# Attention and top-k experts on one core: a later turn of the selection, later copies of the second expert, another order at the end, and identity matmuls in the last sequence

## What is computed

```python
x = _layernorm(x + attention(x, W_key, W_query, W_value, W_proj))   # 16 causal heads of 16
x = _layernorm(x + ffn(x, router_w, w1, b1, w2, b2))
# ffn, for each sequence and each of 8 experts:
scores = softmax(x @ router_w.T)                 # over the experts
gate_vals, sel_idx = top_k(scores_t, capacity)   # capacity 129 of 512 tokens
tokens = x[b_idx, sel_idx]
h = gelu(tokens @ w1 + b1)                       # 256 -> 1024
y = h @ w2 + b2                                  # 1024 -> 256
out = zeros.at[b_idx, sel_idx].add(y * gate_vals[..., None])
```

## Time and profile before

| what | value |
|---|---|
| median of three runs | 898.7 us (894.87, 898.70, 898.88) |
| the profiled execution | 894.26 us; its span 892.5 us, 1.8 us lie around it |
| busy share of the span | PE 92%, DVE 68%, ACT 60%, POOL 52% |
| granted TensorE clock, mean | 0.979 of full |
| attention, until the last scores' turn | about 0 to 409 us |
| end of the last sequence and hand-over | 409 to 480 us |
| experts, steady | 480 to 846 us |
| the end | 846 to 892.5 us |

### The profile page before, as it was taken

How to read it: one execution, slowest core, us unless ns; L and a number is a source line. 1 busy time by engine, 2 the same in 40 slices (tenths; PEclk the granted TensorE clock), 3 DMA queues, 4 the chain that set the end, 5 groups by cost and what they waited for, 6 DMA issues and landing times.

```text
span 892.5 us, 17252 instructions
## 1 busy us (share of the span) xinstructions
PE 821.0 (92%) x5908; PEld 615.5 (69%) x5908; DVE 606.6 (68%) x2067; ACT 532.7 (60%) x1048; POOL 468.0 (52%) x640
## 2 busy tenths in 40 slices
PE   4779999999999999998778999999999999999994
PEld 3534454454645454433258999999999999999993
DVE  5668777788788778899858854546464554646466
ACT  2247767667586766666647445555565656555546
POOL 6458565666655565344658356445444444545343
PEclk9779999999999999999899999999999999999998
DMA  4863434536352424610253223335243342613275
GB/s 144 221 191 112 133 107 151 155 107 185 123 149 95 159 91 156 192 64 11 89 199 109 30 44 60 91 83 145 40 103 69 53 129 40 150 28 52 31 208 188
DMA packets 89574, 100.12 MB, mean 112 GB/s; under 512 B 8592, under 2 KB 82960, under 8 KB 89360
## 3 DMA queue, kind: packets, MB, share of 16 engines
q1 hardware_dynamic: 72128, 77.66, 27.8%
q0 software_dynamic: 12368, 16.52, 11.4%
q10 hardware_dynamic: 4992, 4.85, 1.8%
HBM read 65.38 MB, written 33.23 MB: 110 GB/s over the span
## 4 chain that ended last, share of the span: by engine, by line
PE 72%; DVE 14%; ACT 6%; issue 3%; POOL 1%; DMA 1%; SPq 1%; ACTq 1%; DVEq 0%; POOLq 0%
PE y_ps L1434 22%; PE h_ps L1416 18%; PE av_ps L816 7%; PE st_ps L784 5%; DVE n_ps L648 5%; PE n_ps L799 5%; PE stage_ps L835 3%; PE stage_ps L877 3%; PE stage_ps L843 3%; PE tp_ps L1389 2%; ACT pt L539 1%; DVE nmax L648 1%; DVE best_at L182 1%; DVE row_pool L184 1%; DVE nm L680 1%
## 5 line engine op out<-in xcount | busy, mean ns | idle before, releaser
L648 DVE CUSTOM_DVE_ANT_0 n_ps<-n_ps,tri 128x512 f32<-128x512 f32 (+3 forms) x512 | 238.6, 519 | 72.5 <-PE n_ps L799 70.5
L539 ACT ACTIVATE pt<-st_ps 128x512 f32<-128x512 f32 x320 | 184.4, 602 | 60.5 <-PE st_ps L784 45.5
L1434 PE MATMUL y_ps<-w_parts,h_hi 128*128 128x256 f32 (+1 forms) x1152 | 215.8, 281 | 2.0 <-POOL h_lo L1187 1.6
L1226 ACT ACTIVATE g<-h_ps,b 128x384 f32<-128x384 f32 (+1 forms) x192 | 104.1, 542 | 164.8 <-PE h_ps L1416 138.4
L1434 PEld LDWEIGHTS y_ps<-w_parts,h_hi 128*128 128x128 f32 (+1 forms) x1152 | 172.6, 177 | 5.9 <-issue 1.9
L1416 PE MATMUL h_ps<-tt_hi,w_parts 128*128 128x384 f32 (+1 forms) x768 | 169.7, 323 | 3.7 <-issue 2.0
L1198 POOL DMA_INDIRECT acc<-y,tok_no x61 | 98.1, 1608 | 140.7 <-DVE y L1342 132.7
L1326 DVE TENSOR_TENSOR h_lo<-g,h_hi 128x384 fp32r<-128x384 f32 (+1 forms) x176 | 90.1, 513 | 115.4 <-ACT h_hi L1231 95.6
L468 POOL TENSOR_SCALAR_AFFINE_SELECT pt<-pt 128x256 f32<-128x256 f32 (+1 forms) x320 | 109.8, 361 | 105.4 <-ACT pt L539 104.6
L1434 PE MATMUL y_ps<-w_parts,h_lo 128*128 128x256 f32 (+1 forms) x576 | 161.5, 280 | 0.0
L784 PE MATMUL st_ps<-w_parts 99*128 99x512 bf16 (+3 forms) x512 | 125.7, 307 | 17.5 <-ACT pt L539 15.9
(11 more groups left out here) (209 smaller groups left out, 1091.0 us busy)
## 6 DMA issues: line engine op xcount, KB each, us to landing
w_parts<-part_d SPq DMA_DIRECT2D x186, 128.0 KB, 2.8
w_raw<-in_w SPq DMA_DIRECT2D x16, 1024.0 KB
part_d<-w_raw SPq DMA_DIRECT2D x96, 128.0 KB, 2.2
w_raw<-in_xt SPq DMA_DIRECT2D x8, 512.0 KB, 4.2
res<-in_x SPq DMA_DIRECT2D x8, 512.0 KB, 4.7
x<-res SPq DMA_DIRECT2D x8, 512.0 KB, 3.3
acc<-res SPq DMA_DIRECT2D x8, 512.0 KB, 5.1
fin<-acc SPq DMA_DIRECT2D x4, 512.0 KB, 4.5
```

What stands on the lines that cost most here:

```text
L539: nc.scalar.activation(pt[:, slot % PT_RING, n % UP, :], st_ps[at % ST_RING][:, :], ACT.Exp, scale=S_SCALE).then_inc(exp_done, 1)
L648: ins = nc.vector.tensor_tensor_reduce(out=src[:, h, :], in0=src[:, h, :], in1=mask, scale=-1.0, scalar=-BIG_NEG, op0=ALU.add, op1=ALU.min ...
L1226: nc.scalar.activation(g[:, at % G_RING, 0:cols], h_ps[at % H_RING][:, 0:cols], ACT.Gelu, bias=b1[:, e, n:n + 1]).then_inc(g_done, 1)
L1434: ins = nc.tensor.matmul(y_ps[at % Y_RING][0:rows, 0:C], x[:, q % 2, m, toks], w[e % 2][:, m, :], start=i == 0, stop=i == len(terms) - 1)
```

## The change

Five edits, all in the tables that order the lists, and one new group of instructions.

1. `picked`, `joined` and `fetch` of the early selection go from place 3 to place 7 of the turn behind the last sequence.
2. In the last sequence's turn `lexp` goes from (2, 9) to (3, 8) and `score` from (3, 2) to (3, 9).
3. Expert 1's two copies on ScalarE go from places 1 and 12 to 24 and 25; the rest of its first weight (four VectorE operations, L714 before) moves from that turn to the experts' list, where each piece stands ahead of a piece of `low2`. The load of expert 2's first weight follows it.
4. 40 fp32 matmuls of the identity by itself into a free bank stand ahead of ten `st` stages (2 each) and ahead of `onorm` 2 and 3, `ot` 0 and 1 and `proj` 0 (4, 6, 5, 2, 3) of the last sequence. Their result is not read.
5. At the end the loads of sequences 0, 1, 2 stand ahead of those of 3, 4, 5, the `norm` stages stand elsewhere, and the three `spot` stages are spread over the job.

```diff
+HUM = {("onorm", 2): 4, ("onorm", 3): 6, ("ot", 0): 5, ("ot", 1): 2, ("proj", 0): 3}
+HUM.update({("st", n): 2 for n in range(30, 40)})
...
-NEXT_CUT_AT, NEXT_LOW_AT = ((B, 1), (B, 12)), (B, 11)
-PICK_AT = ((B - 2, 33), (B - 2, 35), (B, 3))
+NEXT_CUT_AT = ((B, 24), (B, 25))
+SCORE_AT = {'lexp': (3, 8), 'score': (3, 9)}
+PICK_AT = ((B - 2, 33), (B - 2, 35), (B, 7))
...
         for stage, b, n in steps():
+            if b == B - 1 and (stage, n) in HUM:
+
+                pe.wait_ge(max_done, B * NU)
+                for _ in range(HUM[stage, n]):
+                    nc.tensor.matmul(n_ps[0][:, 0:P], ident[:, :], ident[:, :], start=True, stop=True)
...
-FINISH += [((NQ - 2, 8), "load", b) for b in (0, 1, 2)]
-FINISH += [((NQ - 1, 0), "norm", 0), ((NQ - 1, 4), "norm", 1)]
...
+FINISH += [((NQ - 2, 8), "load", b) for b in (0, 1, 2) + ON_CHIP]
+FINISH += [((NQ - 2, 8), "norm", 0), ((NQ - 2, 9), "norm", 1), ((NQ - 1, 4), "norm", 2)]
...
             for e in range(1, E):
-                for stage in ("low1", "low2") if e > 1 else ("low2",):
+                for stage in ("low1", "low2"):
...
-        load_w1(2)
```

More of the change, by code:

```diff
@@ L144, in steps @@
                 for gg, kk, stage, ahead, n in STAGES:
+                    if i == B - 1:
+                        gg, kk = SCORE_AT.get(stage, (gg, kk))
                     if (gg, kk) == (g, k) and 0 <= i + ahead < B and (i, stage, n) not in STARTED:
@@ L164, in steps @@
                     yield "cut", 1, NEXT_CUT_AT.index((i, place))
-                if (i, place) == NEXT_LOW_AT:
-                    yield "low", 1, 0
                 if (i, place) == PICK_AT[2]:
@@ L709, in _ @@
                 logits(b)
-            elif stage == "low":
-                hi, lo = weight_parts(ahead, "w1", 1)
-                dve.wait_ge(ahead["w1_top"], 2 * PIECES)
-                for piece in range(PIECES):
-                    nc.vector.tensor_tensor(piece_of(lo, "w1", piece), piece_of(ahead["w1_raw"], "w1", piece),
-                                            piece_of(hi, "w1", piece).bitcast(F32), ALU.subtract).then_inc(ahead["w1_cut"], 1)
             elif stage == "halved":
@@ L935 @@
 ON_CHIP = CHUNKS[JOBS[NQ - 1][1]]
-FINISH = [((NQ - 2, 0), "load", 6), ((NQ - 2, 1), "load", 7)] + [((NQ - 2, 2), "load", b) for b in ON_CHIP]
-FINISH += [((NQ - 2, 4), "norm", 6), ((NQ - 2, 7), "norm", 7)]
-FINISH += [((NQ - 2, 8), "load", b) for b in (0, 1, 2)]
-FINISH += [((NQ - 1, 0), "norm", 0), ((NQ - 1, 4), "norm", 1)]
-ON_CHIP_AT = [((NQ - 2, 0), "spot", b) for b in ON_CHIP]
-ON_CHIP_AT += [((NQ - 1, 7), "spread", ON_CHIP[0]), ((NQ - 1, 8), "spread", ON_CHIP[1]), ((NQ - 1, 8), "spread", ON_CHIP[2])]
-ON_CHIP_AT += [((NQ - 1, 8), "norm", b) for b in (2,) + ON_CHIP]
+FINISH = [((NQ - 2, 0), "load", 6), ((NQ - 2, 1), "load", 7), ((NQ - 2, 2), "norm", 6), ((NQ - 2, 4), "norm", 7)]
+FINISH += [((NQ - 2, 8), "load", b) for b in (0, 1, 2) + ON_CHIP]
+FINISH += [((NQ - 2, 8), "norm", 0), ((NQ - 2, 9), "norm", 1), ((NQ - 1, 4), "norm", 2)]
+ON_CHIP_AT = [((NQ - 3, 1), "place", 0)] + [((NQ - 2, 2 + 2 * n), "spot", b) for n, b in enumerate(ON_CHIP)]
+ON_CHIP_AT += [((NQ - 1, 7), "spread", ON_CHIP[0]), ((NQ - 1, 7), "norm", ON_CHIP[0])]
+ON_CHIP_AT += [((NQ - 1, 8), stage, b) for b in ON_CHIP[1:] for stage in ("spread", "norm")]
 NORMS = [b for _, stage, b in FINISH + ON_CHIP_AT if stage == "norm"]
@@ L1188, in _ @@
                                         h_hi[:, q % 2, n, 0:cols].bitcast(F32), ALU.subtract).then_inc(g_lo, 1)
-            elif stage == "spot" and q == ON_CHIP[0]:
+            elif stage == "place":
                 nc.gpsimd.iota(place[:, :].bitcast(I32), pattern=[[1, T]], base=0, channel_multiplier=0).then_inc(placed, 1)
@@ L1346, in _ @@
                 dve.wait_ge(tp_done, KC * NQ)
-                if n == 0:
+                if q == ON_CHIP[0]:
                     dve.wait_ge(placed, 1)
```

## The result

The changed kernel took 898.1 us (median of 22 runs, 896.37 to 900.44), the kernel before beside it 895.41 us (22 runs, 893.84 to 898.88). The ratio is 1.0024, with a 95% interval of 1.0015 to 1.0032: slower by 2.2 us by the ratio and 2.7 us by the medians, about half of the 0.5% that the text on record takes as the bound for "no difference". The difference is small, but clear of the noise. The profiled execution of the changed kernel took 898.86 us (span 897.1), that of before 894.26 (span 892.5), so the two traces lie 4.6 us apart, more than the medians do.

A forecast was written before the change was run, and what follows sets the result against it. TensorE was taken to bound the kernel from 480 to 846 us, VectorE's norms its end. Terms -0.9 + 3.9 - 2.4 = +0.6 us on a base of 896.7 gave 897.3 us; 8-in-10 range 891.5 to 902.

The forecast's parts named there:

- The sum: Whole kernel: the effects at the last sequence's end, the experts' head and the kernel's end add to +0.6 us.
- the likeliest case: Whole kernel: a measured time within about 0.5%, 4.5 us, of no change; chance 0.61.
- third term: Kernel's end: two norms leave the last stretch, later `spot` stages take some back; -2.4 us, bounds -4.0 and 0.
- first term: End of sequence 7: no held exponential, later turn, identity matmuls keep the clock up; variance 0.9 us earlier, -0.9 us.
- Second term: Head of the experts: four moved weight pieces on full VectorE delay `y`, then GpSimd's `h_lo` and TensorE; +3.9 us.
- 1.44 us for each piece: Experts' head: each of four new VectorE pieces takes 1.44 us beside GpSimd's `h_lo`, 5.8 us in all.
- the first `y` 5.0 us later: Experts' head: VectorE's first `y` comes 5.8 - 0.7 = 5.0 us later, and GpSimd's first scatter-add waits for it.
- TensorE's "3.9 us": `down` of job 1: TensorE stands 5.0 - 1.1 = 3.9 us for GpSimd's late `h_lo`.
- The first rival: Experts' head: the moved pieces' backlog is hidden, costing +0.9 us; sum -2.4 us (894.3); chance 0.22.
- The slip of the first `spread`: Last job: `spot` 4 and 5 delay `y`, so TensorE's first `spread` starts at 872.3 instead of 870.83.
- TensorE ends at 880.8 + 1.4: Kernel's end: TensorE finishes at 882.2, later by 1.4 us; VectorE's last norm ends 1.5 us behind it.
- late loads: Kernel's end: `norm` 2 waits for sequence 2's load, a loss of 2.5 us; sum +5.5 us (902.2); chance 0.13.

The follow-up runs named there:

- after_again: The unaltered changed kernel run once more, on chip 5, against the kernel before: 895.72 us, ratio 1.0040.
- tail_only: The kernel before with only the changed kernel's new order of the end: 894.03 us, ratio 0.9989.
- dve_shift: The changed kernel with 64 already satisfied waits at the head of VectorE's program: 903.44 us, ratio 1.0099.
- both_later: The changed kernel with w2's low parts in job 1, w1's in job 0, and the loads of sequences 3 to 5 early: 895.98 us, ratio 1.0047.
- picks_back: The changed kernel with the early selection's turn back at its earlier place, ahead of the last `av`: 903.29 us, ratio 1.0087.
- gathers_late: The changed kernel with the six gathers of the first two jobs' rows moved behind the last sequence's `rstd` on GpSimd: 905.98 us, ratio 1.0128.
- low2_later: The changed kernel with expert 1's four low parts of w2 moved to job 1: 894.11 us, ratio 0.9980; repeated (_again) on chip 5: 892.24 us, 0.9999.
- loads_early: low2_later with the loads of sequences 3 to 5 two steps into the job before the last: ratio 0.9997 on chip 4, 0.9991 on chip 5.

## Why the prediction was right or wrong

The sum had the right sign (+0.6), but 2.2 us were measured. The figure that came of it had not: 897.3 lies 1.4 us under the 898.7 that stood as the time before, and the kernel became slower. It was built on 896.7 for the kernel before, the middle of two pairs of runs. Over 22 runs that kernel lies at 895.41 with no gap between pairs, so the base was 1.3 us too high, which made up for part of the sum's error: that 897.3 lies only 0.8 us from the 898.1 measured is luck. 898.1 lies within the range, and the likeliest case, no difference, came true. The step that failed is in the third term; the first term is not confirmed; the second is right.

*First term, -0.9.* Its steps hold: no wait of ScalarE, a turn that waits for `av` 31, a clock of 1.00, a projection of 3.8 us. In after_again the projection starts at 455.56 (foretold 455.6) and the variance comes at 460.85 (460.8). The identity matmuls cost a little less than the 0.24 us that I took, 0.22 us each (the five ahead of `ot` start at 451.10, `ot` at 452.21), and those five hid under VectorE.

The gain itself is another matter. Against the variance of sequence 5, the head is 77.96 us in after_again, 1.0 under the 79.00 of before, but these are traces of two chips. And the head is not one number: over the traces with this head it runs from 77.8 to 82.8 us, and tail_only, whose head is before's, has 80.27. What the prediction had no term for is this spread, with holds of 2 to 3 us in some executions and the clock's fall behind them. It made +2.9 of -0.9 in the first trace.

The medians can be asked by subtraction. From a run's difference to the kernel before I take what the lengths of its middle and end differ from before's; the head is left. This is an estimate, good to about 1 us, since the lengths are those of one execution. It gives -0.4 us for the first comparison and -1.1 to +0.2 for the six runs with the whole head on chips 1 to 3 (dve_shift and the runs that alter the head left out). On chips 4 and 5 it gives +0.8 to +1.6 for five runs, +1.0 of them for after_again (both_later left out, whose trace is of the one execution at 889.70 us). So the first term was some -0.5 us on the first chips, which can't be told from -0.9, and by this estimate a loss on the two chips without holds. Why is open.

*Second term, +3.9.* Right, in its size and by its mechanism: 3.7 to 4.2 us by the lengths in seven of nine traces (4.5 and 4.9 in picks_back and gathers_late), 3.7 and 3.8 by the ratios of low2_later (3.5 and 2.5 by the medians). The step "1.44 us for each piece" measured 1.35, "the first `y` 5.0 us later" (5.8 - 0.7 is 5.1) measured 4.4 and 4.7, and TensorE's "3.9 us" measured 3.6 and 3.8 at `down` of job 1, about half of it as a wait in front of the `up` before. The first rival, a hidden backlog, is out. There was a cheap cure that the prediction did not look for: job 1 takes four pieces at 0.69 us each, and in low2_later_again TensorE waits for none of them.

*Third term, -2.4.* This is the term that was mis-sized: -1.2 to -1.4 in the changed kernel's three traces, -1.7 in tail_only's, -1.0 by its ratio. The slip of the first `spread` was foretold (1.3 of 1.4). The step that failed is "TensorE ends at 880.8 + 1.4": from the mark it ended 2.6 us later, not 1.4, since it waited 1.05 us for the load of sequence 5. Less that wait, the term is -2.3; and in loads_early, without the wait, TensorE ended 1.3 us later. The prediction had this mechanism as its rival, late loads, with the landing of up to 9.5 us, but asked it only of sequence 2's load, which `norm` 2 needs; no wait showed there. It is the last load of the row that comes late, and TensorE's last sum needs it. loads_early takes that wait away, has one of 0.66 us on VectorE in its place, and brings the end to -1.9.

Of the 1.6 us between the sum and the measured ratio, then, the end makes about 1.2 and the head about 0.5, and the middle takes 0.2 back.

The Trainium skill, SBUF — State Buffer, section "Who interferes with whom", would have VectorE's pieces, with their two inputs in SBUF, and GpSimd's `h_lo` exclude each other for whole instructions. A pair would then take 0.68 + 0.98 = 1.66 us and the second term would be +4.8. Measured were 1.35 and 1.36 us a pair, so the trace agrees in kind and stays below the rule in size. The piece of 4.05 us beside three `h_lo` of 3.51 together fits an exclusion too, but the rule doesn't say why it should lose to all three, and no run settles that.

## What to carry over

Before filling an idle engine's gap elsewhere, count what the destination already holds: four pieces more cost 3.7 us in a full stretch, and nothing that a trace shows one job later. When several loads are issued in one burst, set the landing time of the last one against its reader, not that of the first: here the last one's wait took up to half of what the new order gave. And for an effect of 2 us, measure lengths between marks in several traces, the kernel before included, and compare only runs of one chip; a single pair of traces here showed +4.6 us for a change of +2.2.

## What I had not expected of the hardware

- A hold of 2 to 3 us on VectorE or ScalarE with releaser "remote", in one execution of a program and not in another of the same program on another chip: 3.60 us from projection matmul to row in the first trace of the changed kernel, 1.17 us in after_again.
- A VectorE operation of 0.69 us took 4.05 when it began 0.02 us behind the first of three GpSimd operations, and 0.69 when both began at 481.09. The executions with these pieces took 897.87 and 889.70 us. That the start decides it is an inference from these two traces, of two kernels on one chip.
- Chips differ by 3 us on this kernel (895.0 to 895.7 and 891.9 to 892.4), and the ratio of the changed kernel to it was 1.0024 in the first comparison and 1.0040 on chip 5; the intervals, 1.0015 to 1.0032 and 1.0028 to 1.0052, overlap a little.
- Four loads issued within 3.0 us on one queue: the slowest landing was 10.6 us, against a median of 4.5 over all DMAs of `acc` there.
